# A transformer layer on one core: the causal mask of the score banks is written by ScalarE instead of TensorE, and VectorE takes maxima and low halves bank by bank

## The reference, cut to what matters

```python
x = x + layernorm(attention(layernorm(x)))          # 8 batches x 512 tokens x 512 channels, 16 heads of 32
x = x + layernorm(ffn(layernorm(x)))                # ternary weights, 512 -> 2048 -> gelu -> 512
...
qkv = x @ w_attn + b_attn                           # q, k turned by RoPE
scores = jnp.einsum('bhtd,bhsd->bhts', q, k)
scores = jnp.where(causal[None, None], scores, -inf)
attn = jax.nn.softmax(scores, axis=-1) * E ** (-0.5)
o = jnp.einsum('bhts,bhsd->bhtd', attn, v)
return o @ w_proj + b_proj
```

## Time and profile before

| | before |
|---|---|
| median of 3 runs | 1350.2 us (1348.36 to 1352.62) |
| the profiled execution | 1350.0 us, of which the span is 1348.2 us |
| PE busy | 89% of the span |
| DVE, ACT, POOL busy | 76%, 58%, 44% |
| mean granted PE clock | 0.955 of full speed |

### The profile page before, as it was taken

How to read it: one execution, slowest core, us unless ns; L and a number is a source line. 1 busy time by engine, 2 the same in 40 slices (tenths; PEclk the granted TensorE clock), 3 DMA queues, 4 the chain that set the end, 5 groups by cost and what they waited for, 6 DMA issues and landing times.

```text
span 1348.2 us, 25057 instructions
## 1 busy us (share of the span) xinstructions
PE 1203.6 (89%) x9388; PEld 652.2 (48%) x9388; DVE 1020.3 (76%) x2931; ACT 780.8 (58%) x1446; POOL 594.2 (44%) x636
## 2 busy tenths in 40 slices
PE   4755889999999999999999999999999999988796
PEld 2322555455545554455545554455545554554343
DVE  7588797868877797878887797868887787777532
ACT  3334864666556664666456755666466755575480
POOL 5231441692049502791149412781159412871252
PEclk9865888999999999999999999999999999999799
DMA  5351121002310113002310113002300221001000
GB/s 203 124 158 57 42 69 55 1 2 56 95 40 3 36 52 102 1 4 66 83 40 2 43 46 102 1 12 68 86 27 3 56 60 44 2 3 55 8 1 31
DMA packets 49685, 65.37 MB, mean 48 GB/s; under 512 B 8439, under 2 KB 33047, under 8 KB 49052
## 3 DMA queue, kind: packets, MB, share of 16 engines
q1 hardware_dynamic: 49564, 63.78, 16.1%
HBM read 29.90 MB, written 8.39 MB: 28 GB/s over the span
## 4 chain that ended last, share of the span: by engine, by line
PE 54%; DVE 30%; ACT 8%; issue 3%; POOL 3%; SPq 1%; DMA 1%; POOLq 0%; DVEq 0%; ACTq 0%
PE gen L476 22%; PE down L519 16%; DVE score L1075 8%; PE pv L573 5%; PE score L545 4%; DVE hT L942 4%; PE score L551 2%; DVE acc_add L1052 1%; POOL rstd L1407 1%; DVE bn L1104 1%; DVE qkn L1167 1%; DVE mx L1075 1%; PE gen L536 1%; DVE probs L942 1%; ACT qkn L736 1%
## 5 line engine op out<-in xcount | busy, mean ns | idle before, releaser
L1407 POOL TENSOR_TENSOR rstd<-veps,mhalf 128x1 f32<-128x1 f32 (+1 forms) x104 | 68.3, 657 | 486.6 <-DVE veps L1152 373.9
L792 ACT ACTIVATE probs<-score 128x512 f16<-128x512 f32 (+1 forms) x384 | 201.9, 526 | 127.4 <-PE score L545 127.4
L942 DVE TENSOR_TENSOR probs<-score,probs 128x512 f16<-128x512 f32 (+1 forms) x384 | 213.2, 595 | 69.2 <-ACT score L794 69.2
L476 PE MATMUL gen<-x2T,t1T 128*128 128x512 f16 x1024 | 242.1, 381 | 5.9 <-DVE hT L942 3.4
L519 PE MATMUL down<-t2T,hT 128*128 128x512 f16 x1024 | 232.9, 380 | 3.5 <-DVE xn L1137 3.5
L794 ACT ACTIVATE score<-score 128x512 f32<-128x512 f32 (+1 forms) x384 | 204.8, 533 | 0.0
L476 PE MATMUL gen<-xT,wa 128*128 128x512 f16 x768 | 180.4, 386 | 11.2 <-DVE wa L962 7.5
L942 DVE TENSOR_TENSOR hT<-gen,hT 128x512 f16<-128x512 f32 x160 | 108.4, 684 | 73.3 <-ACT gen L755 31.6
L1075 DVE CUSTOM_DVE_ANT_0 score<-score,mask_rows 128x512 f32<-128x512 f32 (+1 forms) x344 | 157.6, 519 | 0.0
L519 PEld LDWEIGHTS down<-t2T,hT 128*128 128x128 f16 x1024 | 96.5, 98 | 110.3 <-DVE xn L1137 4.7
L476 PEld LDWEIGHTS gen<-x2T,t1T 128*128 128x128 f16 x1024 | 96.2, 98 | 111.0 <-DVE hT L942 5.3
(11 more groups left out here) (131 smaller groups left out, 1842.2 us busy)
## 6 DMA issues: line engine op xcount, KB each, us to landing
qk<-qkn SPq DMA_DIRECT2D x384, 64.0 KB, 2.0
xo<-x SPq DMA_DIRECT2D x8, 1024.0 KB, 5.7
hT<-x SPq DMA_DIRECT2D x8, 1024.0 KB, 6.4
out<-xn SPq DMA_DIRECT2D x32, 256.0 KB, 2.2
hT<-w_fc SPq DMA_DIRECT2D x4, 1024.0 KB, 6.8
hT<-w_down SPq DMA_DIRECT2D x4, 1024.0 KB, 5.6
hT<-w_attn SPq DMA_DIRECT2D x4, 512.0 KB, 10.1
hT<-w_attn SPq DMA_DIRECT2D x1, 1024.0 KB, 8.7
```

The costliest lines, as they stand in the source:

```text
L476: mm = nc.tensor.matmul(bank[:, :], a, b, start=(start and n == 0), stop=(stop and n == len(pairs) - 1))
L792: nc.scalar.activation(probs[:, h % 2, HI, 512 * i:512 * i + n], score[i][:, 0:n], ACT.Exp, scale=1.0 / S_UP)
L942: return V.tensor_tensor(out, whole, hi, ALU.subtract)
```

## The change

PE no longer multiplies the identity with the mask. ScalarE copies the mask (bf16, 128x128, read four times) into bank 0 in a new function `mask_bank(h)`, with a new semaphore `mask_set`; PE waits for it ahead of `scores(h)` and only adds the four products. For head 0 the copy stands ahead of the exponents of head 0. For head h+1 it stands in `exponents(h)` between the second and the third bank, behind a wait for the low half of bank 0 of head h. On VectorE, in the steps with maxima, the three low halves are no longer behind all maxima; each stands behind the maxima of one bank.

```diff
--- before.py
+++ after.py
@@ -270,7 +270,7 @@
         c_full, c_ready = sem("c_full"), sem("c_ready")
 
         g_full, g_drained = sem("g_full"), sem("g_drained")
-        s_full, s_drained = sem("s_full"), sem("s_drained")
+        s_full, s_drained, mask_set = sem("s_full"), sem("s_drained"), sem("mask_set")
         pv_full, pv_drained = sem("pv_full"), sem("pv_drained")
         down_full, down_drained = sem("down_full"), sem("down_drained")
         hsum_full, hsq_full = sem("hsum_full"), sem("hsq_full")
@@ -547,10 +547,8 @@
                     if h == 0:
                         pe.wait_ge(k_rows, 16)
                         pe.wait_ge(shift_rows, 32 * (j + 1))
-                    bank = claim_score(("scores", h), 0)
-                    nc.tensor.matmul(bank[:, :].rearrange("p (b t) -> p b t", b=TB), identb[:, :],
-                                     mask_b[:, :].unsqueeze(1).to_broadcast([PARTS, TB, PARTS]),
-                                     start=True, stop=False, skip_group_check=True)
+                    pe.wait_ge(mask_set, HEADS * j + h + 1)
+                    bank = score[0]
                     for s in range(TB):
                         mm = part(bank, PARTS * s, s, PARTS * s, PARTS * (s + 1), False)
                     mm.then_inc(s_full, 1)
@@ -785,9 +783,17 @@
                     high(qkn[:, g % 2, 1 + which, :], bank[:, :], bias=qk_bias[:, EC * which + g:EC * which + g + 1]
                          ).then_inc(qk_hi, 1)
 
+                def mask_bank(h):
+
+                    need(act, s_drained, s0 + S["scores", h] - 2)
+                    nc.scalar.activation(blocks(score[0]), mask_b[:, :].unsqueeze(1).to_broadcast([PARTS, TB, PARTS]),
+                                         ACT.Copy).then_inc(mask_set, 1)
+
                 def exponents(h):
 
                     for i, n in enumerate(SCORE_W):
+                        if i == 2 and h + 1 < HEADS:
+                            mask_bank(h + 1)
                         act.wait_ge(s_full, s0 + S["scores", h] + i + 1)
                         nc.scalar.activation(probs[:, h % 2, HI, 512 * i:512 * i + n], score[i][:, 0:n], ACT.Exp,
                                              scale=1.0 / S_UP)
@@ -870,6 +876,7 @@
                         if X_AT[u] + 2 < TB:
                             normalise(X_AT[u] + 2)
                 if here:
+                    mask_bank(0)
                     exponents(0)
                 if nxt and not here:
                     for c in range(EC):
@@ -1058,7 +1065,7 @@
                     dve.wait_ge(h_full, FC * (j - 1) + u + 1)
                     low(hT[:, LO, u, :], bank_of("up", u)[:, :], hT[:, HI, u, :]).then_inc(g_drained, 1)
 
-                def maxima(u, ahead=0, in_general=False):
+                def maxima(u, ahead=0, in_general=False, between=()):
 
                     if in_general:
                         dve.wait_ge(g_full, g0 + G["next max", 3 * u + 2] + 1)
@@ -1076,6 +1083,8 @@
                                                         ALU.max, mx[:, TB * u + tb:TB * u + tb + 1])
                             at += n
                         op.then_inc(g_drained if in_general else s_drained, 1)
+                        if between:
+                            probs_low(between[0], i)
 
                 def halve_maxima():
 
@@ -1169,13 +1178,12 @@
                                            in1=qkn[:, g % 2, 1 + which, :], op0=ALU.add, op1=ALU.subtract
                                            ).then_inc(g_drained, 1)
 
-                def probs_low(h):
-
-                    for i, n in enumerate(SCORE_W):
-                        dve.wait_ge(exp_full, 48 * j + 3 * h + i + 1)
-                        at = 512 * i
-                        low(probs[:, h % 2, LO, at:at + n], score[i][:, 0:n], probs[:, h % 2, HI, at:at + n]
-                            ).then_inc(s_drained, 1)
+                def probs_low(h, i):
+
+                    n, at = SCORE_W[i], 512 * i
+                    dve.wait_ge(exp_full, 48 * j + 3 * h + i + 1)
+                    low(probs[:, h % 2, LO, at:at + n], score[i][:, 0:n], probs[:, h % 2, HI, at:at + n]
+                        ).then_inc(s_drained, 1)
 
                 def head_output(h):
 
@@ -1248,7 +1256,8 @@
                     if not here:
                         hidden_variance()
                 if here:
-                    probs_low(0)
+                    for i in range(3):
+                        probs_low(0, i)
                 if prev:
                     final(0)
                     final_moments(0)
@@ -1288,9 +1297,10 @@
                         final_terms(0)
                     if here:
                         if nxt and h in STEP_MAX:
-                            maxima(STEP_MAX[h], 1, in_general=True)
-                        if h + 1 < HEADS:
-                            probs_low(h + 1)
+                            maxima(STEP_MAX[h], 1, in_general=True, between=(h + 1,))
+                        elif h + 1 < HEADS:
+                            for i in range(3):
+                                probs_low(h + 1, i)
                         head_output(h)
                     if prev and h in FINAL_AT:
                         final_moments(FINAL_AT[h])
```

## The result

The changed kernel takes 1368.38 us (median of 4 runs, 1363.59 to 1369.12), the kernel before beside it 1350.74: a ratio of 1.0127 [1.0111, 1.0144], 17.6 us slower. The forecast was 1358 with a range of 1347 to 1366. The sign came out, and in the usual loops the mechanism and its size too; in the last loop and, less, in the setup loop the forecast missed what was at work. All ratios in this document are of fast executions: one of copy_last (6312 us) and one of the kernel before beside it (1469 us) were slow and are left out.

A forecast was written before the change was run, and what follows sets the result against it. PE bounds the kernel, but in paired steps the chain over ScalarE and VectorE has only 0.26 us to spare and takes over. Usual loops +2.7, last loop +2.1, setup +3.5: +8.3 on 1350.0, so 1358, range 1347 to 1366.

The forecast's parts named there:

- Two steps take 8.18 for 7.93: Usual loops, heads 2 to 5: the chain from scores to weighing becomes the bound, 8.18 us per two steps for 7.93.
- The 0.26 to spare: Usual loops before the change: weighing could have begun 0.26 us sooner, so the chain allowed two steps in 7.67.
- The copy's slot, 0.51: Each mask copy was to take 0.51 us of ScalarE's time, with some 600 ns shown as its duration.
- Steps 6 to 8, +1.12 for the exponents of head 8: Usual loops: the copy for head 8 waits for VectorE's low half of bank 0, making head 8's exponents 1.12 us late.
- Interleave at nothing, the cover needed: Steps 9 to 14: VectorE's new order costs nothing; without its cover each such step loses about copy and bank 2's exponents.
- Usual iteration +0.45: Each of six usual iterations: +1.33 up to the maxima of step 8, -0.88 from heads 10, 11, 14, 15; +2.7 in all.
- Setup +3.5: Setup iteration: a late head 0 and copies between VectorE's low halves in steps 5 and 6 cost 3.5 us, +2 to +4.5.
- From step 8 on nothing changes: Setup iteration: from step 8 on VectorE is full, so no time is gained or lost there.
- The last head loop +2.1: Last loop: ScalarE's 3.02 us per head costs +1.0, +1.5 and +0.8, less 1.2 for six masks ahead of down pieces.
- The clock as a rival at 0.12: Thin loops: more idle PE time lengthens the stretches below full clock, 4 us in each, giving 1366; chance 0.12.
- PE's busy time falls by some 50 us: Whole kernel: PE's busy share was to fall by some 50 us of shown duration while the span grows.

The follow-up runs named there:

- copy_last: The changed kernel with the mask copy behind bank 2's exponents and not ahead of them; 1345.77 us, ratio 0.9982 to the kernel before.
- no_mask: The kernel before without the identity product and with no mask in the maxima either; 1336.50 us, ratio 0.9923.
- copy_narrow: The changed kernel with a mask copy of 128 columns and not 512, other diagonal blocks and the maxima unmasked; 1350.46 us, ratio 1.0021 to before.
- interleave_only: The kernel before with only VectorE's new order of maxima and low halves; 1346.90 us, ratio 0.9996.
- maxima_first: The changed kernel with all maxima ahead of the three low halves, as before the change; 1392.73 us, ratio 1.0327 to before.
- usual_only: The changed kernel with ScalarE's copy in iterations 1 to 6 only, PE multiplying in setup and iteration 7; 1351.22 us, ratio 1.0031 to before.
- warm_narrow: The changed kernel with four extra identity products at nine heads of iteration 7 and GpSimd's squares on 8 of 512 columns; 1360.05 us, ratio 1.0074 to before.
- pool_narrow_before: The kernel before with GpSimd's squares on 8 columns of 512; 1344.29 us, ratio 0.9975.

## Why the prediction was right and wrong

- **Two steps take 8.18 for 7.93**: right (8.14). The 0.26 to spare was measured by no_mask (7.65), the length of the copy by copy_narrow (7.82).
- **The copy's slot, 0.51**: right, 0.52; shown 602 ns, "some 600" was forecast.
- **Steps 6 to 8, +1.12 for the exponents of head 8**: right (+1.16).
- **Interleave at nothing, the cover needed**: right in the usual loops (interleave_only, maxima_first); in the setup loop it gives something back, see there.
- **Usual iteration +0.45**: 72.88-72.07=+0.81 in the loop and -0.16 behind it, +0.65. By usual_only six cost at least 4.2 us for 2.7: the term is somewhat small. One of the six loops took 0.7 more: in iteration 4 the product of step 7 took 3.99 for 2.75.
- **Setup +3.5**: +5.0, above the upper bound of 4.5. Head 0's copy stands at 134.49, exponents at 135.85: 0.35 later than forecast, 0.23 because ScalarE comes to this place later than in the trace before (134.26), the rest because PE waits for the end of the copy (0.59 and 0.15 behind it) and not for its slot. From head 4 to head 7 the loop takes 13.43 for 11.27, +2.2 where I had 1.4 to 2.2. From head 7 to head 8 it takes 7.66 for 6.01, which the forecast had not at all: the product there takes 4.33 for 2.75, as it does in no_mask without any copy (4.45). So some 1.6 of the loss are PE's clock. "From step 8 on nothing changes" was wrong as well: heads 8 to 15 take 37.95 before, 36.16 with VectorE's new order alone and 37.24 with the full change, so the new order gives back 1.8 and the copy takes 1.1 of it. Over all traces, setup loops took 71.7 to 73.3 in four with before's order and PE's mask, 70.5 to 71.5 in four with the new order and PE's mask, and 75.7 to 76.3 in four with the full change.
- **The last head loop +2.1**: this is the step that failed, +7.65. I worked it out from ScalarE's own time alone, 3.02 per head, and the sum had no term for GpSimd and none for the clock. The runs put in its place three parts: some 2 of the chain itself (the remainder of warm_narrow against its partner), the xo product that waits for GpSimd, and down and score products at half clock. Taking away one of the last two gave 0 or 2 us, both gave 3.7: they are not a sum, since with the wait for GpSimd gone the down products took 2.0 longer.
- **The clock as a rival at 0.12**, 1366: nearest to what came, and too low in chance. I priced it as one of several outcomes, beside the forecast, where the forecast's own mechanism brings it on: PE's work gets shorter and its waits longer in the two loops that already stood below full clock. no_mask shows that the first alone is enough.
- **PE's busy time falls by some 50 us**: wrong, it fell by 6.7 (1203.6 to 1196.9). I had read it from the shown 388 ns of each matmul, which overlap with the next; at 0.22 each the products are 27.7, and the lower clock in the thin loops makes others longer.

So the result is 8.3 forecast, 5.55 more in the last loop, 1.5 in the setup, and in this profiled pair -1.2 in the usual iterations (some 3 of luck in it, see the last section) and -0.6 at the end: 13.6.

## What to carry to other kernels

Where an engine's work is moved off, ask step by step which chain is how much shorter than its work; here 0.26 us decided, and 0.5 put in cost more than 0.22 taken out gave. Ask of each operation that will move in time what GpSimd runs beside it: a chain that lengthens can slide into a neighbour's cycle and take on its period. And a thin stretch, in which the bound engine already idles at a lower clock, is to be costed with the clock and the chain together; the same edit can be right in the full stretches and wrong there, so give the choice to each step.

## What the hardware showed that was not expected

A meeting with GpSimd, like that of xo, also makes part of the scatter between executions. Ahead of each head loop VectorE converts a block of maxima to f16. Two iterations of the kernel before, conversion and low half, with GpSimd's first operation:

```profile
431.74 0.22 DVE L1087 CAST m_half<-m_f 64x128 f16<-64x128 f32 x1
431.99 0.28 DVE L942 TENSOR_TENSOR m_half<-m_f,m_half 64x128 f16<-64x128 f32 x1
432.01 1.28 POOL L1431 TENSOR_TENSOR acc_add<-hT 128x512 f32<-128x512 f16 x1
...
580.79 1.15 POOL L1431 TENSOR_TENSOR acc_add<-hT 128x512 f32<-128x512 f16 x1
580.82 1.21 DVE L1087 CAST m_half<-m_f 64x128 f16<-64x128 f32 x1
...
582.06 1.15 DVE L942 TENSOR_TENSOR m_half<-m_f,m_half 64x128 f16<-64x128 f32 x1
```

In the first VectorE comes first by 0.27 and loses nothing; GpSimd's operation takes 1.28 for its usual 1.15. In the second GpSimd is 0.03 ahead, and the two instructions take 1.21 and 1.15. Head 0's exponents then come 78.1 behind head 15's of the iteration before, not 77.0. In pool_narrow_before, with GpSimd's squares narrow, this distance is 76.6 to 77.0 in each of the five such places. Of the profiled pair, before had three such late starts of about 1.1 in these places (and both instructions long once more behind the setup loop, at 281.60, so that the setup's +5.0 is rather too low), after had none. That would be 3 of the 4 us by which the pair is closer than the medians. The other executions have no trace, so whether those of the changed kernel had such late starts is not shown; its profiled one was the shortest of four, 1363.6 for 1367.9 to 1369.1.
